# A mixture-of-experts router fed from raw x: transposes of x before its norm, scales multiplied into the logits, and table rows normalised during the top-k search

## The reference

```
x = x + attn_a(layernorm(x))     # complex linear recurrence over 2048 steps, 64 states
x = x + ffn(layernorm(x))
x = x + attn_b(layernorm(x))     # chunked causal linear attention, 16 heads of 8
x = x + ffn(layernorm(x))

def ffn(x):                      # 4096 tokens, 16 experts, each takes its 256 best tokens
    rms = sqrt(mean(x * x) + 1e-5)
    xn = x / rms * norm_weight
    logits = xn @ router_weight.T + router_bias
    probs = softmax(logits)
    idx = top_k(logits.T, 256)                  # per expert, over all tokens
    h = gelu(xn[idx] @ fc1[e].T + b1[e])
    y = h @ fc2[e].T + b2[e]
    output = scatter_add(y * gate) / sum of the gates of a token
```

## Time and profile before

| what | value |
| --- | --- |
| median of 3 runs | 721.45 us (721.01 to 722.44) |
| profiled execution, its own time | 714.27 us |
| its span on the core | 712.4 us |
| mean granted TensorE clock | 0.762 of full |
| VectorE busy | 435.4 us (61%) |
| TensorE busy | 387.1 us (54%) |
| GpSimd busy | 351.8 us (49%) |
| ScalarE busy | 200.6 us (28%) |

### The profile page before, as it was taken

One profiled execution on the slowest core, in us unless ns is written; L12 is line 12 of the kernel. 1 busy time (PEld: TensorE's weight loads), 2 busy tenths in 40 slices (PEclk: granted clock), 3 DMA queues, 4 the chain that ended last, 5 costly groups with the idle time before them and its releaser, 6 DMA issues.

```text
span 712.4 us, 7685 instructions
## 1 busy us (share of the span) xinstructions
PE 387.1 (54%) x2082; PEld 274.8 (39%) x2082; DVE 435.4 (61%) x1260; ACT 200.6 (28%) x473; POOL 351.8 (49%) x380
## 2 busy tenths in 40 slices
PE   4886664085331597673035666666553314977550
PEld 4554343063110486563012333333332104866540
DVE  6879999986776422221547888888667864221210
ACT  2575000024440242131033333332144402322110
POOL 5048940002001578887308877787420016678853
PEclk9998878597555599998555777888875555999985
DMA  5870000009003133334838899898390031233322
GB/s 143 337 270 0 0 1 0 0 29 267 1 0 44 43 49 44 45 39 71 201 43 129 136 130 118 122 128 124 55 259 0 0 44 47 37 43 44 44 22 18
DMA packets 67397, 55.68 MB, mean 78 GB/s; under 512 B 18017, under 2 KB 55521, under 8 KB 66081
## 3 DMA queue, kind: packets, MB, share of 16 engines
q1 hardware_dynamic: 47744, 44.63, 30.2%
q0 software_dynamic: 11392, 9.05, 9.5%
q10 hardware_dynamic: 8224, 1.57, 1.4%
HBM read 22.73 MB, written 15.73 MB: 54 GB/s over the span
## 4 chain that ended last, share of the span: by engine, by line
DVE 28%; PE 24%; DMA 15%; issue 13%; POOL 10%; ACT 4%; SPq 2%; DVEq 1%; ACTq 1%; POOLq 0%
DVE arena L1137 11%; DMA out<-arena,idx 6%; DMA acc<-arena,idx 5%; POOL acc L526 4%; POOL out L526 4%; PE ps L1075 3%; DVE tk L1142 3%; PE ps L906 2%; DVE arena L1142 2%; PE ps L869 2%; PE ps L1014 2%; DVE arena L1141 2%; PE ps L1101 2%; DVE arena L1520 2%; PE ps L813 2%
## 5 line engine op out<-in xcount | busy, mean ns | idle before, releaser
L1137 DVE TENSOR_TENSOR arena<-ps,arena 128x256 f32<-128x256 f32 (+1 forms) x84 | 34.9, 429 | 140.2 <-DMA acc<-arena,idx 58.5
L719 ACT ACTIVATE arena<-ps,b 128x256 f32<-128x256 f32 x128 | 50.2, 475 | 134.8 <-PE ps L1014 134.8
L1014 PE MATMUL ps<-arena,f1w 128*128 128x256 f32 x256 | 72.3, 433 | 16.6 <-DVE arena L1141 13.2
L589 POOL TENSOR_TENSOR tb<-arena 128x512 f32<-128x512 f32 x64 | 71.0, 1122 | 17.4 <-DVE arena L1520 14.7
L513 POOL DMA_INDIRECT arena<-tab,idx x64 | 62.6, 978 | 33.9 <-issue 18.9
L1024 PEld LDWEIGHTS ps<-f2w,arena 128*128 128x128 f32 x512 | 63.8, 196 | 5.3 <-issue 2.2
L1024 PE MATMUL ps<-f2w,arena 128*128 128x128 f32 x512 | 63.9, 279 | 2.9 <-DVE arena L1141 2.9
L1014 PEld LDWEIGHTS ps<-arena,f1w 128*128 128x128 f32 x256 | 53.0, 218 | 26.4 <-DVE arena L1141 15.0
L526 POOL DMA_INDIRECT out<-arena,idx x32 | 50.9, 1590 | 23.9 <-issue 11.0
L1137 DVE TENSOR_TENSOR arena<-arena 128x256 f32<-128x256 f32 (+21 forms) x107 | 56.0, 558 | 2.2
L526 POOL DMA_INDIRECT acc<-arena,idx x32 | 50.6, 1580 | 10.0 <-issue 6.7
(11 more groups left out here) (250 smaller groups left out, 909.9 us busy)
## 6 DMA issues: line engine op xcount, KB each, us to landing
arena<-arena SPq DMA_DIRECT2D x64, 256.0 KB, 7.2
f1w<-in_f1T SPq DMA_DIRECT2D x4, 1024.0 KB, 12.4
f2w<-in_f2T SPq DMA_DIRECT2D x4, 1024.0 KB, 14.4
tab<-tb SPq DMA_DIRECT2D x8, 512.0 KB, 5.7
acc<-tb SPq DMA_DIRECT2D x8, 256.0 KB, 18.5
arena<-in_f2b SPq DMA_DIRECT2D x2, 1024.0 KB, 5.7
acc<-xs SPq DMA_DIRECT2D x8, 256.0 KB, 6.0
xs<-acc SPq DMA_DIRECT2D x8, 256.0 KB, 5.3
```

Of the source, the lines that this page charges most:

```text
L589: pool.tensor_tensor(by_pairs(QS[:, i, :]), sums_for(i, r), by_pairs(qn[:, r, :]), ALU.mult).then_inc(qs_ready, 1)
L719: last = nc.scalar.activation(hT[:, e % 2, t, :], ps[:, 2 * (e % 2) + t // 2, (t % 2) * CAP:(t % 2 + 1) * CAP], ACT.Gelu, bias=b1[:, e, t: ...
L1014: last = nc.tensor.matmul(ps[:, 2 * (e % 2) + t // 2, (t % 2) * CAP:(t % 2 + 1) * CAP], f1w[:, e, t * P:(t + 1) * P], xeT[:, e % 2, :], st ...
L1137: return nc.vector.tensor_tensor(o, a, b, op)
```

## The change

It touches both feeds, the end of the recurrence and the attention loop.

- The router reads transposed raw x. TensorE transposes groups of `xs` (`transpose_raw`): in the first feed right behind the way out, into the way out's own banks; in the second in the attention loop, group n-2 in turn n, into bank 1. ScalarE copies them to `xT` (`keep_raw`), in the attention loop group n-3 in its turn n, ahead of `norm`.
- The router weights are scaled by `norm_weight` and centred once, before the first feed: two copies on ScalarE and two products with `ident` and `ones` on TensorE. Centred weights drop the mean.
- The token scales `s_r` are widened by VectorE (`cnt`), transposed by TensorE into bank 3 (`spread_scale`), and multiplied into the router's output; ScalarE keeps one factor in `L`. The Exp table is loaded by a one-column Exp ahead of that.
- The table rows leave the path to the logits: GpSimd takes 8 tiles (before 4), ScalarE 4 before the search and 20 in it, one behind each sign count of bits 0 to 9 and 11 to 20; the Exp stands behind bit 10. ScalarE's search is written out instead of looped, and so are VectorE's first ten bits.
- ScalarE copies the transposed logits to `exs`; the row maximum is taken in four parts in bits 0 to 3, the subtraction moves to GpSimd. The first count goes ahead of the shift `evenu`.
- SyncE's stores of the table wait by quarter for these tiles; `acc_in` is merged into `x_in`.

The diff, cut to its core:

```diff
...
+POOL_TILES, EARLY_TILES, EXP_AT = 8, 4, 10
...
                          xs[:, g * TPG:(g + 1) * TPG, :]).then_inc(base_in, 16)
-        sp.wait_ge(normed, NORMED[1 + 2 * f] + ND)
-        sp.wait_ge(normed_pool, (NG - ND) * (f + 1))
+        sp.wait_ge(normed_pool, f + 1)
         for q in range(4):
+            if q:
+                sp.wait_ge(tab_normed, (NT - POOL_TILES) * f + 8 * (q + 1) - POOL_TILES)
             sp.dma_start(tab[f][q * 1024:(q + 1) * 1024, 0:D].rearrange("(t p) w -> p t w", p=P), tb[:, 8 * q:8 * q + 8, 0:D]
...
         pool.wait_ge(zeroed, 16 * NG)
-        pool.wait_ge(normed, NORMED[1 + 2 * f] + 1)
+        pool.wait_ge(shift_ready, 2 * f + 1)
         pool.tensor_copy(ident16, ident[:, :]).then_inc(ident16_ready, 1)
-        for g in range(ND, NG):
-            for j in range(g * TPG, (g + 1) * TPG):
-                last = pool.tensor_scalar(tb[:, j, 0:D], xs[:, j, :], s_mean[:, j:j + 1], s_r[:, j:j + 1],
-                                          ALU.subtract, ALU.mult)
-            last.then_inc(normed_pool, 1)
+        for j in range(POOL_TILES):
+            last = pool.tensor_scalar(tb[:, j, 0:D], xs[:, j, :], s_mean[:, j:j + 1], s_r[:, j:j + 1],
+                                      ALU.subtract, ALU.mult)
+        last.then_inc(normed_pool, 1)
+        ex = exs.rearrange("p (t e) -> p t e", e=NE)
+        pool.wait_ge(lt_kept, f + 1)
+        pool.wait_ge(max_ready, f + 1)
+        pool.tensor_tensor(ex, ex, smx.rearrange("p (t e) -> p t e", e=1).to_broadcast([P, NT, NE]), ALU.subtract
+                           ).then_inc(exp_in, 1)
         pool.wait_ge(exped, f + 1)
-        ex = exs.rearrange("p (t e) -> p t e", e=NE)
         w = NE // 2
...
     roots(NK - 1)
+    act.wait_ge(router_in, 32)
+    act.wait_ge(fb_in, 16 * (2 + NCH))
+    rwf = rwp[:, :, :].rearrange("p i e -> p (i e)")
+    nc.scalar.activation(rws[:, 0, :], rwf, ACT.Copy, scale=nwc[:, 0:1]).then_inc(rw_step, 1)
+    act.wait_ge(rw_step, 1)
+    nc.scalar.activation(rws[:, 1, :], rws[:, 0, :], ACT.Copy, scale=-1.0 / D).then_inc(rw_step, 1)
     inverse(len(UNITS))
...
     last.then_inc(bd_ready, 1)
+    act.wait_ge(rw_prod, 1)
+    nc.scalar.activation(rwf, ps[:, 7, 2 * D:2 * D + 64], ACT.Copy)
     act.wait_ge(mt_prod, 1)
...
+    def keep_raw(f, n):
+        act.wait_ge(raw_T, f * NG + n + 1)
+        if f:
+            to, frm = xT[:, n * GW:(n + 1) * GW], ps[:, 1, :]
+        else:
+            to = xT[:, :].rearrange("p (b t) -> p b t", b=NB)[:, :, 2 * n * P:(2 * n + 2) * P]
+            frm = ps[:, n, :].rearrange("p (b t) -> p b t", b=NB)
+        nc.scalar.activation(to, frm, ACT.Copy).then_inc(rawT_kept, 1)
...
         run = 1 + 2 * f
-        root(run)
-        act.wait_ge(fb_in, 16 * (2 + NCH))
-        for n in range(NG):
-            act.wait_ge(transposed, run * NG + n + 1)
-            nc.scalar.activation(xT[:, n * GW:(n + 1) * GW], ps[:, 6 + n % 2, :], ACT.Copy, scale=nwc[:, 0:1]
-                                 ).then_inc(xT_ready, 1)
-        act.wait_ge(exp_in, f + 1)
-        nc.scalar.activation(exs, exs, ACT.Exp).then_inc(exped, 1)
+        if f == 0:
+            for n in range(NG):
+                keep_raw(f, n)
+                if n == 1:
+                    root(run)
+        else:
+            root(run)
+        nc.scalar.activation(nrm[:, 3:4], ident[:, 0:1], ACT.Exp)
+        act.wait_ge(logit_prod if f else r_spread, f + 1)
+        nc.scalar.activation(L, ps[:, 0 if f else 3, :], ACT.Copy).then_inc(factor_kept, 1)
+        def norm_tile(j):
+            nc.scalar.activation(tb[:, j, 0:D], xs[:, j, :], ACT.Identity, scale=s_r[:, j:j + 1], bias=s_d[:, j:j + 1]
+                                 ).then_inc(tab_normed, 1)
+        act.wait_ge(shift_ready, 2 * f + 1)
+        act.wait_ge(zeroed, 16 * NG)
+        for j in range(POOL_TILES, POOL_TILES + EARLY_TILES):
+            norm_tile(j)
+        act.wait_ge(logit_T, f + 1)
+        nc.scalar.activation(exs, ps[:, 1, :], ACT.Copy).then_inc(lt_kept, 1)
         act.wait_ge(even_ready, f + 1)
-        with act.Fori(0, SPLIT, BITS) as r:
-            for j in range(BITS):
-                act.wait_ge(cand_ready, r + (j + 1 + f * NR))
-                with nc.allow_low_precision(reason="sums of signs up to 256 are exact"):
-                    nc.scalar.activation(eq[:, DCOL:GW], even[:, DCOL:GW], ACT.Sign, bias=tk[:, 0:1], scale=-1.0,
-                                         accum_out=sg[:, 0:1]).then_inc(signed, 1)
+        tile = POOL_TILES + EARLY_TILES
+        for r in range(SPLIT):
+            act.wait_ge(cand_ready, r + 1 + f * NR)
+            with nc.allow_low_precision(reason="sums of signs up to 256 are exact"):
+                nc.scalar.activation(eq[:, DCOL:GW], even[:, DCOL:GW], ACT.Sign, bias=tk[:, 0:1], scale=-1.0,
+                                     accum_out=sg[:, 0:1]).then_inc(signed, 1)
+            if r == EXP_AT:
+                act.wait_ge(exp_in, f + 1)
+                nc.scalar.activation(exs, exs, ACT.Exp).then_inc(exped, 1)
+            elif tile < NT:
+                norm_tile(tile)
+                tile += 1
         if f == 0:
...
             exp_min(k_prod, 5, exk, k_ready, k_neg, k_exp, n)
+        if n >= 3:
+            keep_raw(1, n - 3)
         if n + 2 < NG:
...
     keep_spread(NG - 1)
+    keep_raw(1, NG - 2)
+    keep_raw(1, NG - 1)
     feed(1)
...
+    def transpose_raw(f, n):
+        pe.wait_ge(x3_ready if f else x1_ready, n + 1)
+        if f and n >= 1:
+            pe.wait_ge(rawT_kept, NG + n)
+        for t in range(TPG):
+            j = n * TPG + t if f else (t // 2) * (NT // NB) + 2 * n + t % 2
+            last = nc.tensor.transpose(ps[:, 1 if f else n, t * P:(t + 1) * P], xs[:, j, :], ident[:, :])
+        last.then_inc(raw_T, 1)
+    def route(g):
+        c, i = divmod(g, 2)
+        return nc.tensor.matmul(ps[32 * c:32 * c + 32, 0, :], rwp[:, i, :], xT[:, g * GW:(g + 1) * GW],
+                                start=(i == 0), stop=(i == 1), skip_group_check=True)
+    def spread_scale(f):
+        for q in range(TPG):
+            if q % 2 == 0:
+                pe.wait_ge(r_wide, 2 * f + q // 2 + 1)
+            last = nc.tensor.transpose(ps[:, 3, q * P:(q + 1) * P], cnt[:, q * P:(q + 1) * P], ident[:, :])
+        last.then_inc(r_spread, 1)
...
                      start=True, stop=True).then_inc(mt_prod, 1)
+    pe.wait_ge(rw_step, 2)
+    nc.tensor.matmul(ps[:, 7, 2 * D:2 * D + 64], ident[:, :], rws[:, 0, :], start=True, stop=False)
+    nc.tensor.matmul(ps[:, 7, 2 * D:2 * D + 64], ones[:, :], rws[:, 1, :], start=False, stop=True).then_inc(rw_prod, 1)
     inverse(len(UNITS))
...
     def feed(f):
-        run = 1 + 2 * f
-        for n in range(NG):
-            transposes(run, n, lambda t: tb[:, n * TPG + t, 0:D])
-        pe.wait_ge(router_in, 32)
-        pe.wait_ge(xT_ready, run * NG + NG)
-        for i in range(2):
-            for c in range(4):
-                g = 2 * c + i
-                last = nc.tensor.matmul(ps[32 * c:32 * c + 32, 0, :], rwp[:, i, :], xT[:, g * GW:(g + 1) * GW],
-                                        start=(i == 0), stop=(i == 1), skip_group_check=True)
-        last.then_inc(logit_prod, 1)
+        if f == 0:
+            for n in range(NG - 1):
+                transpose_raw(f, n)
+            pe.wait_ge(rawT_kept, NG - 2)
+            for g in range(0, NG, 2):
+                route(g)
+            transpose_raw(f, NG - 1)
+            spread_scale(f)
+            pe.wait_ge(rawT_kept, NG)
+            for g in range(1, NG, 2):
+                last = route(g)
+            last.then_inc(logit_prod, 1)
+        else:
+            pe.wait_ge(rawT_kept, NG + NG - 1)
+            for g in (*range(0, NG, 2), *range(1, NG - 1, 2)):
+                route(g)
+            pe.wait_ge(rawT_kept, NG + NG)
+            route(NG - 1).then_inc(logit_prod, 1)
+            spread_scale(f)
         pe.wait_ge(logit_ready, f + 1)
...
         pe.wait_ge(ident16_ready, f + 1)
+        pe.wait_ge(lt_kept, f + 1)
         for q in range(TPG):
...
             spread_reciprocals(n - 1)
+        if n >= 2:
+            transpose_raw(1, n - 2)
         if n < NG:
...
         scales(run, 1.0 + EPS, EPS * EPS)
-        dve.wait_ge(zeroed, 16 * NG)
-        for g in range(ND):
-            normalise(run, g, g, lambda t: tb[:, g * TPG + t, 0:D])
+        by_group = s_r.rearrange("p (g q e) -> p q g e", q=TPG, e=1)
+        for q in range(0, TPG, 2):
+            for h in range(2):
+                last = nc.vector.tensor_copy(cnt[:, (q + h) * P:(q + h + 1) * P].rearrange("p (g e) -> p g e", e=NE),
+                                             by_group[:, q + h, :, :].to_broadcast([P, NG, NE]))
+            last.then_inc(r_wide, 1)
+        stt(s_d, s_mean, -1.0, s_r, ALU.mult, ALU.mult).then_inc(shift_ready, 1)
         dve.wait_ge(logit_prod, f + 1)
-        ts(L, ps[:, 0, :], rbc[:, 0:1], None, ALU.add).then_inc(logit_ready, 1)
```

(26 more changed lines are left out.)

46 lines of the change are left out of this document (23 added, 23 removed).

## The result

The changed kernel took **713.18 us** (711.01 to 713.5, 4 runs) where the kernel before took 721.23 (720.77 to 722.44) beside it: a ratio of 0.9883, 95% interval 0.9867 to 0.9899, or 8.05 us less. The direction and the range of the forecast held, the range by 0.8 us; the gain was 3.2 us smaller. Its profiled execution took 713.5 us, with a span of 711.8. That is only 0.6 us less than the span of before (712.4), though the medians differ by 8: the two profiles don't belong to one level of times, as the first experiments show.

What follows compares the result with a forecast made beforehand. No engine holds the kernel; serial waits into both feeds, in the search and attention loop do. -7.6 - 11.25 + 7.2 + 0.4 = -11.25 us, set against the median 721.45: 710.2 us, range 702 to 714.

Steps and rivals of the forecast that it cites:

- First feed: Way into the first search: 28 VectorE tiles and the logit shift leave the path, first bit 7.6 us earlier.
- Second feed: From the last sum into x to the second search: first bit 11.25 us earlier, despite a later Sqrt load.
- Attention loop: ScalarE's wait for raw transposes delays VectorE's division: 2.0 us in three turns, 0.6 in two, 7.2 lost in all.
- Rival B: Attention stall is absent or made up in the loop: -18.45 us, 703.0 us; chance 0.16.
- Search: Both feeds' searches: tiles, Exp, maxima, the saved loop boundary and GpSimd's tiles together cost 0.4 us.
- Tiles free: Twenty tiles per feed in ScalarE's search gaps cost nothing: 0.41 us each against 0.63 idle per bit.
- Maxima 0.8: Four partial row maxima in the search's bits cost 0.1 us per bit, 0.8 in both feeds.
- Saved loop boundary: Search: with the first ten bits out of the loop, one inner boundary goes, minus 1.1 us in both feeds.
- The 0.5 for GpSimd: Second feed: GpSimd's eight tiles beside VectorE's short steps may hold each other, 0 to 3 us, taken as 0.5.
- No cost elsewhere: Router weight centring, covered by 1.7 us before VectorE, later table stores on SyncE and merged semaphores cost nothing.
- Rival C: Table loads or locks on the new path cost more: about -8.05 us, 713.4 us; chance 0.14.
- The other half of C: Instead of stalls behind table loads, GpSimd's tiles block VectorE's setup, costing 3 us.

Runs made afterwards that it cites:

- the first experiments: Kernel before and changed kernel, both unedited, profiled once more: 714.16 and 704.02 us, ratio 0.9851; kernel before a third time, in a series of 721.09 us.
- the version with the tiles behind: Changed kernel with the 20 table tiles of each feed moved from the search's bits to behind them on ScalarE: 704.21 us, ratio 0.9846 to the kernel before.
- the repeated profile: The changed kernel, unedited, profiled once more: 704.02 us, ratio 0.9851 to the kernel before.
- the reordered version: Changed kernel with ScalarE's raw copies in the attention loop put behind its normalisation and reciprocals copy: 696.41 us, ratio 0.9754 to the kernel before; repeated, 702.79 and 0.9741.

## Why the prediction held, point by point

- **First feed, -7.6.** Measured -7.88 and -7.28. The order of ends was right, down to the factor copy that comes last. Up to the logits I had 11.3 us from the last write of x, the traces 11.54 and 12.05. TensorE had idled 2.00 us, and behind that the even router products took 1.50 and 1.94 us (granted clock 0.67 and 0.50) where I took 0.96, and the transposes of group 7 1.11 and 1.12 where I took 0.60. The same 2.00 us stand in the profile of the version with the tiles behind, and there the products ran at a clock of 1.00 and took 1.06; the logits came after 10.75. So this term of the forecast is good to about 1 us, whatever the reasoning. From the logits to the first bit I had 2.7 and got 2.07 and 2.30, which made up for it.
- **Second feed, -11.25.** Measured -11.63 from the last sum into x to the first bit (10.07 against 21.70), and -11.94 with the 9.76 of the repeated profile. The scales' broadcasts took 0.63 for four, not 1.06. The Sqrt load stood behind the last raw copy, as forecast; the root came 0.47 later after the last sum (0.35 forecast), and moving that load gave 0.44.
- **Attention loop, +7.2.** The step held in place, cause and sum: five turns, 7.23 us in the repeated profile (6.0 and 1.2 forecast, 5.76 and 1.47 measured) and 7.2 in the first. The single turns fit less well, 0.5 to 2.6 us in the one profile and 0.1 to 2.7 in the other against 2.0 and 0.6, so that the sum came out so close is in part luck. What my reasons had wrong is the copy's share: I let the copy's 0.6 through by itself, and alone, without the wait, it is made up. Rival B, that the stall would be made up, is out: the reordered version is faster by about the stall, 7.6 us. What the sum lacked is TensorE's clock: a further 2 us in the second turn of one profile and 1.6 from the last turn to the root in the other, where the last numerator's second half (L1156) took 1.78 instead of 1.06 and its own product (L1148) 1.06 instead of 0.60.
- **Search, +0.4.** The sign was right and the parts were wrong. Tiles free: right, shown with and without them. Maxima 0.8: they cost nothing. Saved loop boundary, -1.1 in both feeds: half of it came. The period at the boundary fell from 1.72 to 1.46 us in the first feed and from 1.68 to 1.44 in the second, not to 1.18, and the first ten bits, written out, lose more (their nine periods grew from 10.60 to 11.30 in the first feed). Measured +1.1 for both. The 0.5 for GpSimd was of the right kind: its instructions beside VectorE make single periods longer (1.43 instead of 1.23 in the second search of the repeated profile, where an exclusive or of VectorE took 0.44). It is some 0.3 us in sum, and most of it lies beside the softmax and not beside the tiles.
- **No cost elsewhere.** The centring of the router weights stayed covered, as far as the scatter lets it be seen: from the first root to the last write of x it is 139.4 to 140.7 us in three profiles of before and 139.4 to 141.0 in the others.
- **Rival C (713.4) is nearest to the number, and wrong as a mechanism.** The Exp behind a load started 0.02 us after its end, with no idle time (168.66 and 1.28 end at 169.94, the Exp stands at 169.96), and the copy ahead of the load ended 0.01 before it (168.65). By the rule of the Trainium skill (ScalarE: Activation LUTs, What ACT_TABLE_LOAD costs) a drain of about 1380 ns comes with each switch; neither this pair nor the one in the second feed (the Sqrt load ends at 523.98, the root stands at 524.00) shows it, and the measurement decides. The other half of C, that GpSimd's tiles hold VectorE's setup, did not come up: in the first feed VectorE's scale work is over at 165.07 and the tiles start at 165.52. That the number is C's is chance.
- **The size.** Forecast -11.25, measured -8.05 and, in the other series, -10.1; the intervals of the two ratios overlap. The rows of the table whose forecast is not 0 sum to -9.73 and -9.59, so the steps missed by 1.5 to 1.7 us. At the 714 level: first feed -0.28, second -0.86, loop +1.98, search +0.68; at the 721 level +0.32, -0.59, +1.24 and +0.69. The term that was missing is TensorE's clock in the loop, and the one mis-sized the search. The other rows scatter more than that: the start alone gives -1.01 in one pair and +2.09 in the other, ahead of both feeds. So of the 3.2 us by which the first series missed, these steps hold about half; the rest isn't assigned.

## What to carry to other kernels

Work that fits by size can still cost in full if it waits inside an in-order engine's list: look, for each instruction that you add to a loop, at when its input comes in that same turn and at who needs what is queued behind it; here moving one copy behind the work that VectorE waits for gave back 7.6 us, where the whole change had brought 10.1 in the same series. Where a scale moves behind the product that it scales, ask which short step then ends last; here it was a copy behind a table load behind a late transpose, worth 1.4 to 2.9 us. And compare stages between traces of the same series: two profiles of different levels hid a gain of 8 us.

## What the runs showed of the hardware

- Series of the same kernel differ by a whole per cent as a block: 714.16 and 721 to 722 us for the kernel before. Two traces of it differ by 4.3 us (spans of 714.0 and 718.3): 3.7 us are the stretch from the first gather to the first scatter, in which TensorE's products come one by one with gaps of 0.45 to 1.02 us, and 1.5 the same stretch of the second feed (18.06 against 19.52), where the products run together in both and only start later. All eight profiles at the 721 level have the gaps in the first feed, of either kernel, and none of the five at the 714 level. One chip gave the 714 level and two others the 721 level, with one series each, so it may be the chip; no run here isolates it.
- TensorE's granted clock may rise in the second turn of the attention loop or only after it, for the same program: 1.12 or 2.07 us for the same two products, and 1.7 to 2 us for that turn. Behind the same idle time of 2.00 us in the first feed the same four router products took 1.06, 1.50 or 1.94 us, at granted clocks of 1.00, 0.67 and 0.50.
- Written out on VectorE, the pick of a bit started 0.07 us later than in a loop of one pass, and the loop's first bit started 0.2 us later.
- A VectorE exclusive or on one column, 0.15 us, took up to 0.47 us beside a GpSimd instruction (bits in a loop, second search).
